# Score products on row halves, maxima in twos, and the reciprocals spread by POOL

## The reference

```python
x = x + xattn(layernorm(x), ctx, ctx)      # q, k, v, o projections with biases
#   q = rope(q) * 16 ** -0.5; k = rope(k)
#   scores = q . k over positions idx in [q - 64, q]
#   m = max(scores); e = exp(scores - m); probs = e / sum(e)
#   ctx = probs . v; return ctx @ o_w.T + o_b
x = x + ffn(layernorm(x))                  # top 2 of 8 by router logits
#   per expert: out += mask * ((silu(x @ gw.T) * (x @ uw.T)) @ dw.T) * mean_w
```

## Time and profile before

| | us |
|---|---|
| median of 3 runs | 501.49 (498.05 to 503.87) |
| the profiled execution | 498.88 |
| its span, first to last instruction | 496.9 |
| PE busy in the span | 444.2 (89%) |
| DVE busy | 301.7 (61%) |
| ACT busy | 270.8 (54%) |
| POOL busy | 118.4 (24%) |
| mean granted clock of PE | 0.961 of full speed |

### The profile page before, as it was taken

One profiled execution on the slowest core, in us unless ns is written; L12 is line 12 of the kernel. 1 busy time (PEld: TensorE's weight loads), 2 busy tenths in 40 slices (PEclk: granted clock), 3 DMA queues, 4 the chain that ended last, 5 costly groups with the idle time before them and its releaser, 6 DMA issues.

```text
span 496.9 us, 8810 instructions
## 1 busy us (share of the span) xinstructions
PE 444.2 (89%) x2747; PEld 365.4 (74%) x2747; DVE 301.7 (61%) x727; ACT 270.8 (54%) x853; POOL 118.4 (24%) x118
## 2 busy tenths in 40 slices
PE   3897999999999998309999999999999999999980
PEld 2655675656666654208999999999999999999980
DVE  3664869797887966873746646557376473663330
ACT  1286877787778687404545546455454463643330
POOL 5201014141514214530004041050320402204013
PEclk9999999999999999657999999999999999999995
DMA  7074301020202111157655546554566453213003
GB/s 237 25 209 142 135 22 52 21 64 8 62 12 57 27 41 52 41 153 265 234 160 123 163 105 164 180 98 154 133 149 201 80 168 93 30 39 38 1 1 36
DMA packets 24317, 49.36 MB, mean 99 GB/s; under 512 B 5368, under 2 KB 15160, under 8 KB 24140
## 3 DMA queue, kind: packets, MB, share of 16 engines
q10 hardware_dynamic: 7886, 26.44, 17.2%
q1 hardware_dynamic: 10238, 15.36, 10.3%
q0 software_dynamic: 6144, 6.97, 8.6%
HBM read 38.51 MB, written 12.74 MB: 103 GB/s over the span
## 4 chain that ended last, share of the span: by engine, by line
PE 73%; DVE 7%; ACT 6%; issue 4%; POOL 3%; DMA 3%; SPq 2%; ACTq 1%; POOLq 0%; DVEq 0%
PE b_o L634 9%; PE b_small L634 9%; PE b_s L621 8%; PE b_s L622 8%; PE b_s L623 8%; PE b_s L420 6%; ACT probs L749 4%; PE b_pv L443 3%; PE b_pt L621 3%; PE b_pt L623 3%; PE b_pt L622 3%; PE b_pt L429 3%; PE b_proj L474 3%; PE b_proj L498 2%; PE b_s L418 2%
## 5 line engine op out<-in xcount | busy, mean ns | idle before, releaser
L749 ACT ACTIVATE probs<-b_s,negmax 100x100 f32<-100x100 f32 x256 | 85.6, 361 | 24.1 <-DVE negmax L1003 21.2
L1191 POOL DMA_INDIRECT out<-y_sb,idnow x32 | 48.7, 1522 | 180.5 <-ACT y_sb L790 173.1
L778 ACT CAST h_hi<-h_sb 128x448 fp32r<-128x448 f32 x64 | 36.3, 567 | 86.5 <-DVE h_sb L1094 86.5
L621 PE MATMUL b_s<-x_hi,w_hi 128*128 128x448 f32 x192 | 72.2, 376 | 0.7 <-DVE x_lo L1084 0.7
L622 PE MATMUL b_s<-x_lo,w_hi 128*128 128x448 f32 x192 | 71.3, 371 | 0.0
L623 PE MATMUL b_s<-x_hi,w_lo 128*128 128x448 f32 x192 | 71.1, 370 | 0.0
L981 DVE TENSOR_TENSOR w_lo<-w_raw,w_hi 128x1024 fp32r<-128x1024 f32 x48 | 58.4, 1224 | 13.6 <-ACT w_hi L713 13.6
L1098 DVE TENSOR_TENSOR h_lo<-h_sb,h_hi 128x448 fp32r<-128x448 f32 x64 | 40.2, 628 | 40.5 <-ACT h_hi L778 40.5
L749 ACT ACTIVATION_READ_ACCUMULATOR probs<-b_s,negmax 100x1 f32 x256 | 57.1, 223 | 0.0
L420 PE MATMUL b_s<-kblk,qrot 128*100 128x400 f32 x128 | 53.7, 500 | 0.0
L1003 DVE TENSOR_REDUCE negmax<-b_s 100x4 f32<-100x400 f32 x64 | 36.2, 566 | 27.0 <-PE b_s L420 26.3
(11 more groups left out here) (131 smaller groups left out, 930.2 us busy)
## 6 DMA issues: line engine op xcount, KB each, us to landing
w_raw<-in_ffw ACTq DMA_DIRECT2D x48, 512.0 KB, 3.9
xin<-slots SPq DMA_DIRECT2D x9, 449.8 KB, 4.6
slots<-in_padrows SPq DMA_DIRECT2D x8, 449.8 KB, 4.6
kblk<-krot SPq DMA_DIRECT2D x128, 12.5 KB, 1.8
out<-x_all SPq DMA_DIRECT2D x8, 200.0 KB
ctx_all<-in_ctxT SPq DMA_DIRECT2D x1, 1200.0 KB, 6.3
x_all<-in_x SPq DMA_DIRECT2D x1, 1200.0 KB
attw<-in_wT ACTq DMA_DIRECT2D x2, 256.0 KB, 3.7
```

The lines of the kernel that those rows point to most:

```text
L621: pe.matmul(o, wh[:, c, cols], x_hi[:, c, :], start=(c == 0), stop=False)
L749: m = nc.scalar.activation(probs[:, N % 3, h, :], b_s[N % 3][0:S, h * S:(h + 1) * S], ACT.Exp, bias=negmax[:, N % 4, h:h + 1], accum_out=p ...
L778: nc.scalar.copy(h_hi[:, f, :], h_sb[:, f % 2, :]).then_inc(s_hhi, 1)
L1191: G.indirect_dma_start(out, bass.IndirectOffsetOnAxis(idnow[:, n:n + 1], 0), y_sb[:, n, :], None, bounds_check=TOK + TILE - 1, oob_is_err= ...
```

## The change

The score product of a quad uses one half of the rows: the keys of heads 0 to 3 of a chunk lie in rows 0 to 63 and those of heads 4 to 7 in rows 64 to 127, both in the same 400 columns, so `kblk` has half the size. At even slots PE issues the masks of two quads and then their two products; at odd slots it issues none. DVE takes both maxima at even slots. The k projection and its evacuation move from slot 1 to slot 0, `k_rotate` from slot 2 to 1, `places` from slot 5 (before `q_rotate`) to slot 6 (after the maxima). `den` on DVE keeps the reciprocal, and POOL makes the copy in a new function `spread`. In `rows_write` one copy writes the row numbers of both batches.

```diff
@@ -186,7 +186,7 @@
         swap = att_sb("swap", [P, 2, DC * 2, S])
         krot = att_sb("krot", [P, DC * 2, S])
         qrot = att_sb("qrot", [P, 2, DC * 2, S])
-        kblk = att_sb("kblk", [P, 2, DC, HC, PT])
+        kblk = att_sb("kblk", [P, 2, DC, QH, PT])
         v_sb = att_sb("v_sb", [S, 2, 2, D])
         probs = att_sb("probs", [S, 3, QH, S])
         rdenx = att_sb("rdenx", [S, H, DH])
@@ -266,6 +266,7 @@
         s_pT = sem("s_pT")
         s_pTc = sem("s_pTc")
         s_pv = sem("s_pv")
+        s_rden = sem("s_rden")
         s_rx = sem("s_rx")
         s_rT = sem("s_rT")
         s_rTc = sem("s_rTc")
@@ -341,7 +342,7 @@
                 for c in range(DC):
                     for h in range(HC):
                         r = slice(h * DH, (h + 1) * DH)
-                        sp.dma_start(kblk[r, i % 2, c, h, :],
+                        sp.dma_start(kblk[r, i % 2, c, h % QH, :],
                                      krot[r, 2 * c:2 * c + 2, :].rearrange("p b s -> p (b s)")
                                      ).then_inc(s_kblk[c], 16)
 
@@ -404,22 +405,25 @@
                 return n // (H // QH), n % (H // QH)
 
             def scores(i, n):
-                N = NQ * i + n
                 b, s = quad(n)
                 c = s * QH // HC
-                h = s * QH % HC
                 if n == 0:
                     pe.wait_ge(s_qrot, i + 1)
                 if n in (0, HC // QH):
                     pe.wait_ge(s_kblk[c], 16 * HC * (i + 1))
-                if N >= 3:
-                    pe.wait_ge(s_p, N - 2)
-                o = b_s[N % 3][0:S, 0:QH * S]
-                pe.matmul(o, ident_bf[0:S, 0:S], mask_bf[0:S].rearrange("p h s -> p (h s)"),
-                          start=True, stop=False)
-                pe.matmul(o, qrot[:, i % 2, 2 * c + b, :],
-                          kblk[:, i % 2, c, h:h + QH, b * S:(b + 1) * S],
-                          start=False, stop=True).then_inc(s_s, 1)
+                banks = []
+                for m in range(2):
+                    N = NQ * i + n + m
+                    if N >= 3:
+                        pe.wait_ge(s_p, N - 2)
+                    banks.append(b_s[N % 3][0:S, 0:QH * S])
+                    pe.matmul(banks[m], ident_bf[0:S, 0:S], mask_bf[0:S].rearrange("p h s -> p (h s)"),
+                              start=True, stop=False)
+                for m in range(2):
+                    r = slice(m * P // 2, (m + 1) * P // 2)
+                    pe.matmul(banks[m], qrot[r, i % 2, 2 * c + b, :],
+                              kblk[r, i % 2, c, :, b * S:(b + 1) * S],
+                              start=False, stop=True).then_inc(s_s, 1)
 
             def probs_transpose(N):
                 pe.wait_ge(s_p, N + 1)
@@ -562,7 +566,7 @@
                     for m in ((N - 4,) if n % 4 == 0 else (N - 3,) if n % 4 == 2 else ()):
                         if 0 <= m < NQ * NPAIR:
                             values(m)
-                    if cur:
+                    if cur and n % 2 == 0:
                         scores(i, n)
                     if n == 5 and 0 <= i - 2 < NPAIR:
                         ranks(i - 2)
@@ -580,7 +584,7 @@
                         o_project(2 * i - 2)
                     if n == 6 and nxt:
                         v_project(i + 1)
-                    if n == (0 if i < 0 else 1) and nxt:
+                    if n == 0 and nxt:
                         k_project(i + 1)
                     if n == 1 and nxt:
                         xn_transpose(i + 1)
@@ -894,10 +898,7 @@
 
             def den(r):
                 v.wait_ge(s_p, 4 * r + 4)
-                link(V.reciprocal(rden[:, r % 2, :], psums[:, r % 2, :]))
-                if r:
-                    v.wait_ge(s_rT, r)
-                V.tensor_copy(rdenx[:, :, :], bc(rden[:, r % 2, :].unsqueeze(2), [S, H, DH])).then_inc(s_rx, 1)
+                V.reciprocal(rden[:, r % 2, :], psums[:, r % 2, :]).then_inc(s_rden, 1)
 
             def attend(r):
                 b = r % 2
@@ -926,8 +927,9 @@
                 v.wait_ge(s_rstd2, i + 1)
                 if i >= 2:
                     v.wait_ge(s_scat[i % 2], 16 * TOPK * 2 * (i // 2))
+                V.tensor_copy(xrow[:, i % 2, :, D:RW].rearrange("p b w -> p (b w)").bitcast(I32),
+                              rows_sb[0:S, 2 * i:2 * i + 2])
                 for b in range(2):
-                    V.tensor_copy(xrow[:, i % 2, b, D:RW].bitcast(I32), rows_sb[0:S, 2 * i + b:2 * i + b + 1])
                     ins = V.tensor_scalar(xrow[:, i % 2, b, 0:D], x_all[:, 2 * i + b, :], mv2[:, b, 0:1],
                                           rstd2[:, b:b + 1], ALU.subtract, ALU.mult)
                 ins.then_inc(s_xr, 1)
@@ -996,12 +998,12 @@
                     N = NQ * i + n
                     if n == 3 and 0 <= i - 2 < NPAIR:
                         choose_masks(i - 2)
-                    if cur:
-                        v.wait_ge(s_s, N + 1)
-                        if N >= 4:
-                            v.wait_ge(s_p, N - 3)
-                        V.tensor_reduce(negmax[:, N % 4, :],
-                                        b_s[N % 3][0:S, 0:QH * S].rearrange("p (h s) -> p h s", h=QH),
+                    for M in (N, N + 1) if cur and n % 2 == 0 else ():
+                        v.wait_ge(s_s, M + 1)
+                        if M >= 4:
+                            v.wait_ge(s_p, M - 3)
+                        V.tensor_reduce(negmax[:, M % 4, :],
+                                        b_s[M % 3][0:S, 0:QH * S].rearrange("p (h s) -> p h s", h=QH),
                                         AX.X, ALU.max, negate=True).then_inc(s_max, 1)
                     if n == 0 and nxt:
                         xn_write(i + 1)
@@ -1009,7 +1011,7 @@
                         den(2 * i - 1)
                     if n == 2 and prv:
                         attend(2 * i - 1)
-                    if n == (0 if i < 0 else 2) and nxt:
+                    if n == (0 if i < 0 else 1) and nxt:
                         k_rotate(i + 1)
                     if n == 0 and i == NPAIR + 1:
                         for k in range(2):
@@ -1022,10 +1024,10 @@
                         residual(i - 1)
                     if n == 5 and cur:
                         den(2 * i)
-                    if n == 5 and 0 <= i - 2 < NPAIR:
-                        places(i - 2)
                     if n == 5 and nxt:
                         q_rotate(i + 1)
+                    if n == 6 and 0 <= i - 2 < NPAIR:
+                        places(i - 2)
                     if n == 6 and cur:
                         attend(2 * i)
                     if n == 6 and prv:
@@ -1151,6 +1153,12 @@
                         G.indirect_dma_start(slots, bass.IndirectOffsetOnAxis(desti[:, i % 2, c:c + 1], 0),
                                              xrow[:, i % 2, b, :], None).then_inc(s_scat[i % 2], 16)
 
+            def spread(r):
+                g.wait_ge(s_rden, r + 1)
+                if r:
+                    g.wait_ge(s_rT, r)
+                G.tensor_copy(rdenx[:, :, :], rden[:, r % 2, :].unsqueeze(2).to_broadcast([S, H, DH])).then_inc(s_rx, 1)
+
             g.wait_ge(s_zero, 2)
             for i in range(-1, NPAIR + 2):
                 if i + 1 < NPAIR:
@@ -1162,7 +1170,10 @@
                     xs = x_all[:, 2 * i + 2:2 * i + 4, :]
                     G.tensor_tensor(xs, xs, biasrow[:, 1:2, :].to_broadcast([S, 2, D]), ALU.add).then_inc(s_xob, 1)
                 if 0 <= i - 1 < NPAIR:
+                    spread(2 * i - 1)
                     inverse_deviation(i - 1, s_var2, mv2, ve2, rstd2, s_rstd2, s_xr)
+                if 0 <= i < NPAIR:
+                    spread(2 * i)
                 if 0 <= i - 2 < NPAIR:
                     scatter(i - 2)
                 if i + 2 < NPAIR:
```

## The result

| | before | after |
|---|---|---|
| median of 4 runs each, us | 501.64 | 512.74 |
| lowest to highest | 498.05 to 503.87 | 510.03 to 518.38 |
| ratio, 95% interval | | 1.021 [1.013, 1.030] |
| the profiled execution; its span | 498.88; 496.9 | 512.46; 510.6 |
| first mask to last exp's end | 174.8 | 186.4 |

What follows compares the result with a forecast made beforehand. PE sets the pace at 22.5 us a pair; afterwards the places-scatter chain binds at 22.3. Savings along the pairs sum to 6.6 us, less 1.4 at the end: net 5.2, median 496.3 us, range 489 to 502.

Steps and rivals of the forecast that it cites:

- the part on `places`: places a slot later delays desti, POOL's scatter and the deviation behind it; PE stalls some 2 us in pairs 2 to 5.
- The chain of 22.3 us: Desti, scatter, deviation, xn, PE's slots 2 and 3, DVE, places: 22.3 us per pair, with a 2 us wait before xn_transpose.
- rival 1: Scatter doesn't bind, L457 shows no wait; pairs 2 to 5 take 20.4 us too, 488.7 in all; chance 0.20.
- DVE's 7.1 us: DVE's part of the chain: two maxima, residual, reciprocal, q_rotate, two maxima and places, 7.1 us.
- The double slot: Two masks, then two half-row products side by side: 1.28 us, saving 0.48 per two quads, 1.9 per pair.
- the k move: k projection a slot earlier: 1.38 us of PE wherever it stands; pair 1's key DMAs start earlier.
- this loop: ACT's double-slot loop, 4.4 us where PE first needs the copied quad (slots 2 and 6); binds only in the last pair.
- The 20.5 of PE's own work: PE's own work per pair in the changed kernel, 20.5 us, against the chain's 22.3.
- Pairs 0, 1 and 7: Savings: pair 0 1.7 us as key DMAs land earlier, pair 1 0.8 with six w_raw issues delaying ACT, pair 7 1.3.
- spread(15) behind the scatter: At the end, spread(15) waits on POOL behind scatter(5), so attend comes 4.5 us after the last exp, not 3.0: 1.4 lost.
- The spread on POOL: POOL's copy of the reciprocals takes 0.6 us, hidden by 0.25; at 1.27 it would cost 0.4 per pair.
- The single write for the row numbers: One of two row-number copies goes from rows_write, which stands behind the chain: saves nothing.

Runs made afterwards that it cites:

- experiment 1: Changed kernel with places back in slot 5 before q_rotate: 502.57 us, ratio 1.005; kernel before with only places moved to slot 6: 508.04, 1.017.
- experiment 7: Changed kernel with POOL's inverse_deviation of pair i+2 put ahead of the scatter of pair i-2: 524.87 us, ratio 1.045.
- the faster kernel: Changed kernel with places in slot 5, q_rotate at the end of slot 3 and w_raw's loads issued one a slot: 495.79 us, ratio 0.991 to the kernel before.
- experiment 9: Reruns: changed kernel unedited 519.79 us; kernel before unedited 499.38; changed kernel with places, q_rotate and w_raw loads mended 495.79; kernel before with loads spread 497.20.
- its counterpart: Kernel before, with full rows, and only w_raw's loads issued one a slot: 497.20 us, ratio 0.995 to the kernel before.
- experiment 4: Row halves and maxima in twos alone: 500.84 us, ratio 1.002; changed kernel with k moves undone: 513.63, 1.024; with spread back on DVE: 517.04, 1.033.
- experiment 8: w_raw's loads one a slot: changed kernel, places slot 5, q_rotate slot 3, 496.03 us; kernel before 498.95; kernel before with q_rotate in slot 3 507.46.
- the first kernel of experiment 4: Row halves and maxima in twos alone; k projection, its evacuation, k_rotate, places and spread as in the kernel before: 500.84 us, ratio 1.002.
- experiment 2: Changed kernel with PE's ranks moved from slot 5 to behind v_project in slot 6, places left in slot 6: 514.82 us, ratio 1.033.

## Why the prediction was wrong

**The step that failed** is the part on `places`. It followed what comes behind desti, POOL's scatter and the deviation, and not what waits for the first instruction of `places`, the read of `b_small`. I followed the chain behind the step that moves and not the bank in front of it. That is PE's 1.42 us in front of L510 in pairs where I had forecast none there. In the kernel before, the move with this wait and with attend behind places costs 8 us; in the changed one its undoing gives 8 back, of which some 3 are the late slot 0 (experiment 1). No rival had it; the range ended at 502, and pairs forecast at 22.3 us took 23.3 and 24.4.

**The chain of 22.3 us** was built right in its first part (xn waits 1.29 for rstd; the scatter ends right before) and wrong in what it does: PE reaches xn_transpose no earlier, so moving xn by 1.6 us changed nothing (experiment 7). I forecast a wait of 2 us at that transpose; there was none. That was my sign for rival 1, and the pairs did not take its 20.4 us either: that PE does not wait for one chain says nothing of the others. The loop that did close went over DVE to attend and values, an exit that my sum of DVE's 7.1 us did not name.

**The double slot** was right: 1.28 forecast, 1.33 measured, and the products side by side. Its gain, 0.43 each or 1.7 us a pair, reaches the pair only as 0.6. The stretches of the faster kernel in experiment 9, against its counterpart, show where: slots 2-3 gain 0.3 and slots 6-7 0.4; slots 0-1 and 4-5 gain nothing (6.6 for 6.5, 4.6 for 4.6), as ACT's copies end last there. PE's timeline in that kernel, at the end of slot 1 and in slot 5:

```profile
110.55 0.99 PE L447 MATMUL b_pv<-probsT,v_sb 100*32 100x200 f32 x8
111.47 0.54 PE L420 MATMUL b_s<-mask_bf,ident_bf 100*100 100x400 bf16 x2
...
120.58 0.53 PE L447 MATMUL b_pv<-probsT,v_sb 100*32 100x200 f32 x4
121.74 0.53 PE L447 MATMUL b_pv<-probsT,v_sb 100*32 100x200 f32 x4 [0.62 <-ACT probsT L733]
```

Eight passes of values take 0.92 us from start to start where they took 0.48: the second four stand behind ACT's copy, which begins at 110.42, right behind ACT's evacuation of k (109.79). With k_project left in slot 1 slots 0-1 took 6.17 (experiment 4), 0.35 less than before, so the k move, which I had cost PE nothing, took this stretch's gain back. No run has the faster kernel with k in slot 1. In slot 5 the wait has a name and is 0.62. I had this loop in the text, at 4.4 us, and said that it binds only in the last pair, since a pair takes 20 us or more. That compares a sum over the pair; slots 4-5 hold no projection, and there it binds in every pair. The 20.5 of PE's own work was never to be had.

**Pairs 0, 1 and 7.** Pair 0 gained 0.6 for 1.7. Pair 1 was to gain 0.8 and lost 2.2: PE waited 0.9 us longer behind the burst of loads, and the clock fell behind it, which it did in some runs behind shorter waits too and not behind every longer one (experiment 8). In pair 7 the bank cost again: L510 waits 0.83 us for `place` there. At the end, 1.4 us were to be lost by spread(15) behind the scatter; 1.9 were, but by another cause. It ran at 208.7, well ahead of PE's L510 at 210.93, and the run with the spread on DVE and old places (experiment 4) has the same tail, 4.9 us. The granted clock was at 0.56 and 0.59 in the two windows from 206 to 210 us, around and behind the last exp (206.87), and whole in the kernel before; the o projection, PE's timelines, after and before:

```profile
206.42 1.92 PE L522 MATMUL b_o<-attw,att 128*100 128x256 f32 x4
```

```profile
194.51 1.03 PE L518 MATMUL b_o<-attw,att 128*100 128x256 f32 x4
```

**The spread on POOL** (0.6 forecast, 0.4 measured) cost nothing that the runs show. The single write for the row numbers was not tried alone.

**What stays open** is the cause of the late slot 0, about 1.1 us in each of pairs 4 to 6. It is not the increments, not k_project in that slot (7.26 without it), not POOL's spread (7.47 without it in pairs 4 and 5). A late scatter does not bring it by itself either. In pair 3 of the changed kernel the four DMAs run from 1.9 us ahead of the pair's first mask to 3.3 behind it, in pair 4 from 1.9 ahead to 3.1 behind, and only pair 4 is late (6.44 and 7.53). With the ranks moved (experiment 2) they run from 1.4 ahead to 3.6 behind in pair 4, and slots 0-1 took 6.50 in pairs 4 to 6; in the kernel before with places in slot 6 they took 6.52. And the kernel before with the loads spread showed the lateness in pairs 4 and 5 of one profile (7.67, 7.63) and in none of another. So it can come without any part of the change.

## What to carry to other kernels

Before a step is moved, list who waits for its first instruction as well as for its last: a shared bank or buffer that it reads is held until then, and the writer is often on the busiest engine. A gain on the busiest engine counts only in the stretches where that engine ends last, so sum it by stretches between two waits and not over the whole period. And a burst of DMA issues, or any longer idle time of PE, is paid twice if the clock falls behind it; spread over slots, six loads gave each kernel 2 to 4 us in that pair.

## What the hardware showed that I had not expected

- Two fp32 products on 64 rows each, 400 columns in two passes, run in two rounds of 0.42 us (118.51 and 118.93), 0.85 us in all up to the next product, against 0.67 for one product on 128 rows. Four transposes right behind them took 0.40 us from start to start (111.83 to 112.23) where they took 0.34 before.
- At one and the same place, PE's wait for xnT in pair 1, the clock was at half behind waits of 1.47 us (the first kernel of experiment 4), 1.91 and 2.83, and whole behind 1.90 and 1.97 (both profiles of the kernel before), 2.53 and 2.64 (experiment 4, spread on DVE). The length of the one wait does not tell which it will be.
- An engine that waits for PE can go on as late as 1.57 us behind the end that PE's rows show (ACT's copy in pair 4 of the changed kernel; 0.16 in pair 3), with no gap in PE's rows at that point; whether the signal or the shown end is at fault is not known.
- A copy with a broadcast input, 100x256, takes 0.40 us on POOL (median of 16), where DVE took 0.25 (0.49 less the reciprocal's 0.24).
